# A decoder layer on one core: the opening's splits, stores and fetches in a new order over two DMA queues, and weights as the standing operand of the routed experts

## The reference

```python
x = x + attn(layernorm(x))       # 16 batches of 128 tokens, 256 wide
x = x + xattn(layernorm(x), ctx, ctx)
x = x + ffn(layernorm(x))

# attn: differential attention, 16 heads of 2 x 8
o = softmax(q1 k1') v - lam * softmax(q2 k2') v
o = o * rsqrt(mean(o * o) + EPS) * subln_w * (1 - LAMBDA_INIT)
return o @ W_proj + b_proj
# xattn: one head over ctx, then gelu and ctx as residual
# ffn: a shared SwiGLU (hidden 1024) plus 2 of 16 routed experts (hidden 256)
h = silu(x @ w1[e]) * (x @ w2[e])
y = (h @ w3[e]) * gate[e]
```

## Time and profile before

| | us |
|---|---|
| median of 3 runs | 619.63 (618.93 to 621.52) |
| the profiled execution, its own time | 615.97 |
| its span in the profile | 614.7 |
| TensorE busy | 555.1 (90%) |
| VectorE busy | 315.2 (51%) |
| GpSimd busy | 229.1 (37%) |
| ScalarE busy | 221.7 (36%) |
| chain that ended last | PE 35%, issue 19%, DMA 12%, SP's queue 11%, POOL 10%, DVE 9% |

### The profile page before, as it was taken

How to read it: one execution, slowest core, us unless ns; L and a number is a source line. 1 busy time by engine, 2 the same in 40 slices (tenths; PEclk the granted TensorE clock), 3 DMA queues, 4 the chain that set the end, 5 groups by cost and what they waited for, 6 DMA issues and landing times.

```text
span 614.7 us, 10001 instructions
## 1 busy us (share of the span) xinstructions
PE 555.1 (90%) x3310; PEld 336.1 (55%) x3310; DVE 315.2 (51%) x681; ACT 221.7 (36%) x414; POOL 229.1 (37%) x473
## 2 busy tenths in 40 slices
PE   8967879899879877799999899997999999999998
PEld 6534336445546443575586456474666656666447
DVE  5749775597795995855242661111222222223282
ACT  7314544564554645615512200101333333333110
POOL 2534575455744554312010024562333333333100
PEclk9978979799998979899999999998999999999999
DMA  7651675232322138960039705222222232322731
GB/s 210 203 154 54 192 224 175 89 107 81 96 74 70 44 136 75 223 179 1 0 97 349 239 17 198 77 94 71 78 88 87 86 87 87 87 86 68 267 112 51
DMA packets 62192, 72.39 MB, mean 118 GB/s; under 512 B 14816, under 2 KB 55264, under 8 KB 60608
## 3 DMA queue, kind: packets, MB, share of 16 engines
q1 hardware_dynamic: 58352, 61.37, 35.5%
q0 software_dynamic: 3792, 10.39, 4.8%
HBM read 45.31 MB, written 26.03 MB: 116 GB/s over the span
## 4 chain that ended last, share of the span: by engine, by line
PE 35%; issue 19%; DMA 12%; SPq 11%; POOL 10%; DVE 9%; ACT 3%; POOLq 0%; DVEq 0%; ACTq 0%
PE ps L589 13%; DMA x_slots<-XN,slot_i 7%; POOL y_rows L1544 7%; PE ps L600 5%; SPq L1681 3%; SPq L1667 3%; PE ps L421 3%; SPq L1659 3%; PE ps L519 2%; DVE nmax L853 2%; DMA pack_k<-qk_parts 2%; PE ps L500 2%; SPq L1689 2%; PE ps L388 1%; POOL goes_to L1538 1%
## 5 line engine op out<-in xcount | busy, mean ns | idle before, releaser
L853 DVE TENSOR_REDUCE nmax<-ps 128x8 f32<-128x1024 f32 x64 | 77.8, 1217 | 41.5 <-PE ps L388 41.1
L644 PE MATMUL ps<-W,xt 128*128 x188 | 90.3, 603 | 1.2 <-ACT xt L1375 1.0
L1544 POOL DMA_INDIRECT y_rows<-yo,goes_to x47 | 45.8, 975 | 91.5 <-DVE yo L1086 91.5
L1279 ACT ACTIVATE prob<-ps 128x1024 f32<-128x1024 f32 x64 | 65.4, 1023 | 39.0 <-PE ps L409 39.0
L1079 DVE TENSOR_TENSOR sa<-sa,ps 128x256 f32<-128x256 f32 x47 | 19.8, 421 | 97.6 <-ACT sa L1382 97.6
L589 PE MATMUL ps<-xT,W1s 128*128 128x512 f32 x128 | 64.0, 624 | 2.4 <-ACT sil L1368 0.9
L589 PE MATMUL ps<-xT,W2s 128*128 128x512 f32 x128 | 60.9, 598 | 0.0
L600 PE MATMUL ps<-W3s,hTs 128*128 128x256 f32 x256 | 56.5, 381 | 3.5 <-DVE hTs L1012 3.5
L1368 ACT ACTIVATE sil<-ps 128x512 f32<-128x512 f32 x32 | 19.1, 597 | 106.8 <-PE ps L589 88.9
L1012 DVE TENSOR_TENSOR hTs<-sil,ps 128x512 f32<-128x512 f32 x32 | 22.0, 688 | 67.6 <-PE ps L589 63.5
L600 PEld LDWEIGHTS ps<-W3s,hTs 128*128 128x128 f32 x256 | 48.2, 190 | 13.2 <-DVE hTs L1012 5.1
(11 more groups left out here) (184 smaller groups left out, 877.0 us busy)
## 6 DMA issues: line engine op xcount, KB each, us to landing
W<-in_L_ffn_routed_w_dram SPq DMA_DIRECT2D x12, 1024.0 KB, 11.9
qk_parts<-part SPq DMA_DIRECT2D x28, 256.0 KB, 3.4
pack_q<-qk_parts SPq DMA_DIRECT2D x48, 128.0 KB, 3.1
pack_k<-qk_parts SPq DMA_DIRECT2D x48, 128.0 KB, 3.1
xg<-x_slots SPq DMA_DIRECT2D x47, 129.0 KB
x_slots<-zero SPq DMA_DIRECT2D x11, 512.0 KB, 11.1
yg<-y_rows SPq DMA_DIRECT2D x4, 1024.0 KB, 8.5
X<-in_x_dram SPq DMA_DIRECT2D x4, 512.0 KB, 7.6
```

The costliest lines, as they stand in the source:

```text
L644: r = t.matmul(ps[:, 2 + p, :], xt[:, p, k, :], W12[:, ds(e, 1), k, :].rearrange("p o f -> p (o f)"), start=(k == 0), stop=(k == KT - 1))
L853: v.tensor_reduce(nmax[:, s % 4, a, :, :], ps[:, b:b + 2, :].rearrange("p m (h t) -> p m h t", h=4), AX_X, ALU.max, negate=True).then_inc( ...
L1279: a.activation(prob[:, n:n + 2, :], ps[:, 2:4, :], ACT.Exp, scale=HD ** -0.5).then_inc(exped, 1)
L1544: g.indirect_dma_start(out=y_rows, out_offset=bass.IndirectOffsetOnAxis(ap=goes_to[:, n:n + 1].bitcast(U32), axis=0), in_=yo[:, p, :], in_ ...
```

## The change

**Opening.** The tiles of a chunk are made in the order of `ORDER`: queries then keys of heads 0 to 7, and only then those of heads 8 to 15. Chunk 0 is stored in halves (`store_half`, 14 DMAs of 128 KB, each issued as its part is ready, with a semaphore for each half), and unit 0 needs only half 0. Its six key fetches are issued by ScalarE (`fetch_keys`), between its copies of chunk 1's xT and chunk 1's first splits; SP issues the six of the queries. The first scores stand right behind the second chunk's projections. The third chunk's last two tiles move into step 0, the fourth chunk's turn to step 1, its four tiles and their stores one step later. Eight loads of `Wp` move from before the stores to step 3; the eight loads of `sub_c` become one of `sub_row`, from which VectorE makes `sub_c`. The single semaphore of the later loads becomes four.

**Routed stage.** ScalarE copies w1 and w2 of tile n + 3's expert to one of three buffers (`copy_weights`), with the expert's number now in its own register. `raise_` takes the weights as the standing operand and x as the moving one, in pieces of 128 columns, so that its result has the orientation that `lower` needs: `flip` and `put_h` are gone, and VectorE writes the product straight to `ht`.

```diff
-TURN_AT = (0, 0)
-QK_AT = ((1, 0), (2, 0), (3, 0), (4, 0))
+THIRD_CHUNK_AT = ((0, 0), (0, 1))
+TURN_AT = (1, 1)
+QK_AT = ((2, 0), (3, 0), (4, 0), (5, 0))
...
-WF_AT, A_AT, B_AT, M_AT = (5, 0), (6, 0), (7, 0), (7, 1)
+WF_AT, A_AT, B_AT, M_AT = (5, 1), (6, 1), (7, 0), (7, 1)
...
+ORDER = (0, 2, 1, 3)
...
                 if a == 0:
                     t.wait_ge(packed[u], 16 * FETCHES * (s // CB // UNITS + 1))
+                if n < 2:
+                    t.wait_ge(rests, 6 + 2 * n)
...
             def raise_(n):
                 p = n % 2
-                e = t.value_load(expert_of[0:1, n:n + 1], min_val=0, max_val=NE - 1)
                 t.wait_ge(xt_put, n + 1)
                 if n >= 2:
                     t.wait_ge(r_gated, n - 1)
-                for k in range(KT):
-                    r = t.matmul(ps[:, 2 + p, :], xt[:, p, k, :], W12[:, ds(e, 1), k, :].rearrange("p o f -> p (o f)"),
-                                 start=(k == 0), stop=(k == KT - 1))
+                t.wait_ge(r_copied, n + 1)
+                for h in range(2 * RH // P):
+                    for k in range(KT):
+                        r = t.matmul(ps[:, 2 + p, h * P:(h + 1) * P], Wn[:, n % 3, k, h * P:(h + 1) * P], xt[:, p, k, :],
+                                     start=(k == 0), stop=(k == KT - 1))
                 r.then_inc(r_raised, 1)
-
-            def flip(n):
...
+            def fetch_keys(unit):
+                half = unit % 2
+                a.wait_ge(k_ones, unit + 1)
+                a.wait_ge(halves_stored[half], 16 * STORES)
+                for r0, p0 in enumerate(K_RUNS):
+                    for m in range(2):
+                        a.dma_start(Kp[unit][MG * m + r0:MG * m + KQ:3, :, :].rearrange("p h t -> p (h t)"),
...
-            def put_h(n):
...
+            def copy_weights(n):
+                e = a.value_load(expert_of[0:1, n:n + 1], min_val=0, max_val=NE - 1)
+                if n >= 3:
+                    a.wait_ge(r_raised, n - 2)
+                a.activation(Wn[:, n % 3, :, :].rearrange("p k f -> p (k f)"),
+                             W12[:, ds(e, 1), :, :].rearrange("p o k f -> p (o k f)"), ACT.Copy).then_inc(r_copied, 1)
...
+            put_turned(norm, 1, 4, xT)
+            fetch_keys(0)
+            for i in range(4):
+                put_first(1, i)
...
                 if n + 3 < NT:
                     put_x(n + 3)
+                    copy_weights(n + 3)
                 if n + 2 < NT:
                     act_routed(n + 2)
-                put_h(n + 1)
...
+            def store_half(half, i):
+                for n, (f0, at_) in enumerate(PARTS_AT[i]):
+                    f = f0 + half
+                    q.wait_ge((firsts, seconds, thirds)[i], ORDER.index(f) + 1)
+                    q.dma_start(qk_parts[0, f, at_, :, :, :].rearrange("d m t -> (d m) t"),
+                                part[0][:, i, f, :]).then_inc(halves_stored[half], 16)
...
             for i in range(3):
-                store_part(0, i)
-            fetch(0, range(PIECES))
+                store_half(0, i)
+            for i in range(2):
+                store_half(1, i)
+            fetch(0, range(PIECES - len(K_RUNS)))
+            store_half(1, 2)
             for s in range(LEAD - 1):
                 fetch(1, range(3 * s, 3 * s + 3))
+                if s == 0:
+                    store_part(1, 0)
                 put_max(s)
+            store_part(1, 1)
             for s in range(STEPS):
                 if s + LEAD - 1 < STEPS:
                     put_max(s + LEAD - 1)
-                if s in (0, 3):
+                if s == 0:
+                    store_part(1, 2)
+                if s == 3:
+                    for j in range(4):
+                        for i in range(2):
+                            r0 = 32 * j + VD * i
+                            load(Wp[r0:r0 + VD, :, :],
+                                 W_proj.rearrange("(a i j d) n -> i j d a n", i=2, j=4, d=VD)[i, j], head_weights_in)
+                if s == 4:
                     for i in range(3):
-                        store_part(1 + s // 3, i)
+                        store_part(2, i)
```

More of the change, by code:

```diff
@@ L152, in decoder_layer @@
         sub_c = small.put("sub_c", [P, 1])
+        sub_row = small.put("sub_row", [P, VD])
         lam = small.put("lam", [P, 4, HD])
@@ L269, in decoder_layer @@
         parts_stored = [sem(f"parts_stored{c}") for c in range(NC)]
+        halves_stored = [sem(f"halves_stored{h}") for h in range(2)]
         packed = [sem(f"packed{u}") for u in range(UNITS)]
@@ L785, in tensor_program @@
             raise_(1)
-            flip(0)
             for n in range(NT - 1):
@@ L791, in tensor_program @@
                     raise_(n + 2)
-                flip(n + 1)
                 lower(n)
@@ L948, in between @@
             def between(s, a):
+                if s == 0 and a == 0:
+                    stats(norm, 3, 3)
+                if s == 0 and a == 1:
+                    split(2, 2)
+                if s == 1 and a == 0:
+                    split(2, 3)
+                    normalize(norm, 3, 3, xn)
                 if (s, a - 1) in QK_AT:
                     subtract_first(3, QK_AT.index((s, a - 1)))
+                if (s, a) == WP_AT:
+                    prepare_weights()
                 if (s, a) == LIFT_AT:
@@ L1459, in scalar_program @@
             a.wait_ge(experts_known, 1)
-            put_x(0)
-            put_x(1)
-            act_routed(0)
-            put_x(2)
-            act_routed(1)
-            put_h(0)
+            a.wait_ge(routed_in, 16 * 3 * (NE // EL))
+            a.wait_ge(shared_added, CB * (NC - 1))
+            for n in range(3):
+                copy_weights(n)
+                put_x(n)
+                if n:
+                    act_routed(n - 1)
             for n in range(NT - 1):
@@ L1488, in add_bias, with put_third @@
                 g.tensor_tensor(X[:, b, :], X[:, b, :], bp_b[:, :], ALU.add).then_inc(bp_added, 1)
-            def put_third(c, f):
-                g.wait_ge(seconds, 4 * c + f + 1)
-                if c == 2 and f == 0:
-                    g.wait_ge(parts_stored[0], 16 * STORES)
-                g.tensor_tensor(part[PART_OF[c]][:, 2, f, :], rest[:, f % 2, :], part[PART_OF[c]][:, 1, f, :], ALU.subtract).then_inc(thirds, 1)
+            def put_third(c, i):
+                f = ORDER[i]
+                g.wait_ge(seconds, 4 * c + i + 1)
+                if c == 2 and i == 0:
+                    for half in range(2):
+                        g.wait_ge(halves_stored[half], 16 * STORES)
+                g.tensor_tensor(part[PART_OF[c]][:, 2, f, :], rest[:, i % 2, :], part[PART_OF[c]][:, 1, f, :],
+                                ALU.subtract).then_inc(thirds, 1)
             def split_max(s):
@@ L1553, in between @@
             def between(s):
+                if s == 0:
+                    scale(norm, 3)
+                    put_third(2, 2)
+                if s == 1:
+                    put_third(2, 3)
                 if (s - 1, 0) in QK_AT:
@@ L1656, in sync_program, with load @@
             cv = ctx_1024.rearrange("b p d -> p b d")
-            def later(dst, src):
-                q.dma_start(dst, src).then_inc(later_in, 16)
+            def load(dst, src, into):
+                q.dma_start(dst, src).then_inc(into, 16)
             def row(w, n):
```

256 lines of the change are left out of this document (139 added, 117 removed).

## The result

| | before | after |
|---|---|---|
| median, us | 620.49 (618.93 to 621.52, 4 runs) | 611.38 (609.49 to 612.52, 4 runs) |
| profiled execution, own time | 615.97 | 611.33 |
| its span | 614.7 | 610.1 |
| chain that ended last | PE 35%, SP's queue 11%, DVE 9% | PE 42%, SP's queue 1%, DVE 11% |

The ratio of the runs is 0.9881, with a 95% interval from 0.9852 to 0.991. Measured again later (e8, ten runs) it was 0.9857, 0.9812 to 0.9901. So the change makes the kernel 1.2 to 1.4% faster, by these ratios 7 to 9 us, where I forecast 603 and a range that ended at 611.0.

The account below looks back on a forecast made before the run. SP's queue was taken to bound the opening, half steps to pace the steps, TensorE the routed stage. Profiled 615.97 - 8.2 (opening and steps) - 8.5 (routed stage) = 599.3 us; median forecast 603, range 598 to 611.

Parts of the forecast that it names:

- Step 1: Opening: SP free earlier, keys land earlier, first scores at 30.4 us, step 0 near 48, 7.3 us earlier.
- Step 2: Steps 0 and 1: projection tiles moved in cost 2.7 us and chunk 3's turn 1.5, leaving 3.1 us of lead.
- Step 3: Near step 6: the maxima's wait and slow half go, 5.0 us gained together with the lead; stall at unit 3's keys stays.
- Step 4: Routed stage: a tile takes 2.85 us instead of 3.03, 8.5 us over 47 tiles, with ScalarE's work hidden.
- (c): Routed stage: weight loads don't overlap their products, +1.6 us a tile, +73 us, 685; chance 0.02.
- (a): The routed gain comes, the opening's doesn't: keys delayed or SP's waits move one step; 609, chance 0.22.
- (b): Routed stage slower: ScalarE becomes the bound at the weight copy and register load; some 642 at 2 us; chance 0.06.
- (d): Opening gains more than counted because TensorE never goes cold there; 11 + 10 us, 599, chance 0.08.

Follow-up runs that it names:

- e8: The changed kernel itself measured again later, without further edits, in ten runs against the kernel before; ratio 0.9857 (0.9812 to 0.9901).
- e3: The changed kernel with VectorE's lift of the query weights moved from step 5 into the opening; 604.9 us, ratio 0.9753.
- e5: The changed kernel with the lift moved to the opening and unit 3's keys fetched ahead of the fourth chunk's stores; 602.4 us, ratio 0.9745.
- e4: The changed kernel with SP's five stores of the fourth chunk moved behind unit 3's last four key fetches; 605.8 us, ratio 0.9792.
- e7: e5 without TensorE's wait for the last routed tile's result before the shared expert's last chunk; 598.6 us, ratio 0.9676.
- e9: e7 with the six first key fetches issued by SP behind the queries', not by ScalarE; 599.2 us, ratio 0.9691.
- e12: e7's kernel measured again in more rounds; 599.9 us, ratio 0.9679.
- e14: e7 plus the fourth chunk's statistics moved to the opening and its normalisation to step 0's first half; 596.0 us, ratio 0.9641.
- e10: The changed kernel with ScalarE's copy of the weights made a second time per routed tile, into an unread buffer; 609.6 us, ratio 0.9829.
- e13: e14 plus ten more transposes of the identity on TensorE before the first turn; 595.2 us, ratio 0.9637.

## Why the prediction was wrong

**Step 1, the first keys: in parts right.** SP was free at 14.65 (forecast 14), ScalarE issued six fetches in 3.8 us (as taken), step 0 started at 47.59 (48). The first scores came at 33.69 and not at 30.4. The clock in the first chunk moved the fetches back by about 1.7 us, but it isn't the main cause: where it held, the first scores came at 31.87 to 34.70. The main cause is the landing, taken as 3.1 us from the earlier trace rows and measured at 5.5 here, at 5.3 to 6.5 in the other traces with two queues. The row was read where one queue was at work. The error was made good behind it: from the first scores to step 0 I counted 17.5 us, it took 13.9.

**Step 2, the moved work: wrong in size.** 1.5 us for the turn, bounded by 3. The stretch came out 2.1 us over the forecast in this trace, and 1.6 on average in eleven. I priced TensorE's work and VectorE's queue, but not that the turn stands directly behind the end of VectorE's normalisation, nor that this takes 1.55 us in some executions and 2.6 in others, nor that the clock falls behind the idling.

**Step 3, SP in the steps: this is the step that failed.** That "the wait of 3.27 us is gone but for half a microsecond, and with it the slow half behind it" had SP's side right: e3 shows a wait of 0.47 us and the stretch at 8.06. What I put at nothing without looking is what is late next. The rows were in the trace of before: VectorE's lift ended at 87.2, 0.7 us before the wait did, and the maxima behind it at 88.33, after it. Of 5.0 us 0.8 came. With the lift moved (e3) the stretch is 4.1 us shorter than before. The price of the slow half was too high as well: I took 3.1 us for it at full clock, a half with a projection tile, but this one has the products by `Wraw` and takes 3.8 without its wait (e3, e5), so 1.5 us and not 2.2. That SP's last four fetches for unit 3 would end near 99 and land at 102.3 failed too: they ended at 105.44, and the first scores came at 108.97. I let SP's list run at its own pace, but its place there is behind the maxima of step 9, which TensorE gives (98.35), and behind five stores. e3 and e4 show both terms as separate, and e5, e7, e9 and e12 to e14 have both gains.

**Step 4, the routed stage: right in the steady state, its end missing.** 2.85 against 2.87 for the tile, 0.111 as read in the earlier trace rows, ScalarE and its register load hidden, with 0.26 us for the latter (0.3 taken). The Trainium skill ("TensorE: Matmul & The Clock Gate", "The mechanism") says that loads overlap products in flight only when their row groups differ, which would give (c); the trace does not agree, since 752 loads that all fill the 128 rows overlap their products here. The same section also says that a load into the background weight buffer is pulled ahead of products in flight; the trace is not at odds with that, though no run shows such a buffer. The term was 8.5; the stage gave 7.8, and 1.7 was given back behind it by the clock. The six traces without the wait show that it is the wait: 3.6 us or more, with what it cost before.

**The rivals.** (a), 609, was the nearest: the routed gain comes, the opening's doesn't. Its reason was partly right, "SP's waits only move one step"; in truth one moved to VectorE and one stayed. (b) was further off than I thought (e10). (c) did not come. Nor did (d): TensorE went cold in new places.

**The sum** is off by 8.2 + 8.5 - 9.1 = 7.6 us on the medians, and by 16.7 - 4.6 = 12.1 between the two profiled executions. There it is 4.2 at step 6, 2.1 at the turn, 0.7 from (2,1) to (5,1), 0.9 at unit 3, 0.7 in the 47 tiles, 1.7 at the tail, 2.2 between the steps and the routed stage, less 0.4 at step 0. The 2.2 have no edit behind them; I put them down to what the clock did in this execution, since the products by `M_T` at 245 us took 6.03 us in after and 3.72 in before, each behind 0.84 us of idling. Over the sixteen traces it is 179.2 to 182.1 us from the last half to the routed stage, and before's is the shortest. In three of the sixteen the stretch (10,1) to (31,1), which the change doesn't touch, takes 127 us, in the others 121.3 to 124.7.

**A faster version.** With the four edits of e14 the kernel takes 596.0 us, 3.6% under the kernel before (ratio 0.9641, 0.9609 to 0.9674), where the change alone has 1.2 to 1.4%; with e13's transposes 595.2.

## What to carry to other kernels

When a wait is removed, list what every other engine does during it, with the time at which each ends, and take the gain only back to the one that ends last: here VectorE's lift ended 0.7 us before the wait, and the maxima behind it 0.4 us after. Work that lies under a stall is free only as long as the stall is there, so move both, as e3 does. A wait on TensorE costs more than itself where the clock falls behind it: here 1.9 us of idling cost 1.7 more, at the tail and at the start.

## What the runs showed of the hardware

Two DMA queues with fetches of 128 KB did not bring them sooner than one (first scores at 33.06 us in e12, 33.23 in e9): the DMA engines' share goes from 0.84 to 1.0, the rate stays at some 190 to 240 GB/s, and a fetch on the second queue takes 5.3 to 6.5 us to land instead of 3.4 in e9. ScalarE's instructions behind one another are 0.95 us apart where each lasts 1.06, and 0.31 where each lasts 0.38, so that a sum of durations overrates its load by a tenth or more. Where the register load stands in its list, ScalarE idles 0.26 us. VectorE's normalisation of the fourth chunk, the same four instructions each time, took 1.55 to 1.73 us in four traces and 2.51 to 2.62 in seven.

TensorE's clock fell from 2.4 to 1.2 GHz behind 1.83, 1.93 and 2.06 us of idling ahead of the first turn, and there not behind 1.56 or less (ten traces). It fell behind the 1.66 us near step 6 in five traces of five (the scores or the products behind it show it), behind 1.86 to 3.24 us at the routed stage's tail in eight of eight, and not behind 0.84 there in before. Before `M_T` it idled 0.84 us each time, and the products behind it were slow in four of sixteen traces.
